# In the heads, TensorE turns a tile's own rows and makes its queries one head step sooner in its order

## What is computed

```
h = einsum('bnc,hdc->bhnd', x, Wh)            # 4 heads, 64 features
scores = where(mask, einsum('...nd,...md->...nm', h, h), NEG)
out_h = einsum('...nm,...md->...nd', softmax(scores), h) + bh
z = leaky_relu(concat_heads(out_h), 0.2)
h2 = einsum('bnk,dk->bnd', z, Wo)             # goes on to a second attention
```

## Time and profile before

| | |
|---|---|
| median of 3 runs | 1794.92 us (1794.16 to 1799.05) |
| the profiled execution | 1795.05 us |
| its span, first to last instruction | 1793.2 us |
| granted TensorE clock, mean over the span | 0.858 |
| PE busy | 1080.2 us, 60% |
| DVE busy | 1308.8 us, 73% |
| POOL busy | 1035.0 us, 58% |
| ACT busy | 784.8 us, 44% |

### The profile page before, as it was taken

How to read it: one execution, slowest core, us unless ns; L and a number is a source line. 1 busy time by engine, 2 the same in 40 slices (tenths; PEclk the granted TensorE clock), 3 DMA queues, 4 the chain that set the end, 5 groups by cost and what they waited for, 6 DMA issues and landing times.

```text
span 1793.2 us, 13782 instructions
## 1 busy us (share of the span) xinstructions
PE 1080.2 (60%) x3144; PEld 558.8 (31%) x3144; DVE 1308.8 (73%) x1699; ACT 784.8 (44%) x2502; POOL 1035.0 (58%) x939
## 2 busy tenths in 40 slices
PE   0000255365289899869999985646534777764673
PEld 0000132122144444434444441212113444542231
DVE  7987456789699997994768505999976986734462
ACT  0400253334247566544655652536433546643131
POOL 0084437641167788657686656877744865415882
PEclk9999988687699899979999998877775889876886
DMA  9260547431222122101111004442204543206666
GB/s 339 74 117 20 198 153 207 136 114 48 94 62 80 41 66 64 53 12 30 42 41 36 12 12 143 131 114 84 87 24 138 149 137 96 70 34 186 199 186 160
DMA packets 101626, 178.81 MB, mean 100 GB/s; under 512 B 47552, under 2 KB 56032, under 8 KB 99232
## 3 DMA queue, kind: packets, MB, share of 16 engines
q0 software_dynamic: 30960, 102.92, 19.9%
q1 hardware_dynamic: 51216, 70.05, 11.8%
q10 hardware_dynamic: 19360, 4.87, 1.6%
HBM read 147.88 MB, written 34.12 MB: 101 GB/s over the span
## 4 chain that ended last, share of the span: by engine, by line
DVE 30%; PE 29%; POOL 19%; issue 11%; ACT 5%; DMA 4%; DVEq 0%; POOLq 0%; ACTq 0%; SPq 0%
PE PS L1230 15%; POOL big L654 10%; DVE big L1691 5%; DVE big L1683 3%; PE PS L1176 3%; PE PS L1254 2%; PE PS L1290 2%; ACT big L897 2%; PE PS L1242 2%; DVE big L1687 2%; DVE big L1570 2%; POOL big L682 2%; DVE big L1617 2%; DVE stats L1613 2%; DVE big L1489 2%
## 5 line engine op out<-in xcount | busy, mean ns | idle before, releaser
L1230 PE MATMUL PS<-big,ident 128*128 128x512 f32 x1044 | 507.5, 637 | 107.1 <-ACT big L897 45.2
L897 ACT ACTIVATE big<-big 128x64 f32<-128x64 f32 x1632 | 404.7, 339 | 241.8 <-DVE big L1648 202.6
L682 POOL TENSOR_TENSOR big<-big 128x512 f32<-128x512 f32 x356 | 361.5, 1045 | 134.8 <-DVE big L1648 113.0
L1230 PEld LDWEIGHTS PS<-big,ident 128*128 128x128 f32 x1044 | 209.7, 206 | 367.4 <-issue 269.4
L1691 DVE TENSOR_REDUCE big<-big 128x32 f32<-128x2048 f32 (+4 forms) x126 | 297.7, 2362 | 4.3
L1214 PE MATMUL PS<-big,ident 128*128 128x512 f32 x348 | 190.3, 708 | 153.7 <-ACT big L897 85.8
L1683 DVE TENSOR_TENSOR big<-big,PS 128x2048 f32<-128x2048 f32 (+4 forms) x84 | 198.5, 2363 | 80.9 <-PE PS L1242 78.1
L654 POOL DMA_INDIRECT big<-tab,SI x142 | 174.2, 1227 | 117.7 <-PE PS L1214 40.9
L1176 PE MATMUL PS<-ident,big 128*128 128x128 f32 x640 | 105.8, 295 | 167.8 <-DMA big<-h_rows 67.8
L689 POOL TENSOR_TENSOR big<-big 128x512 f32<-128x512 f32 x64 | 81.5, 1273 | 147.7 <-ACT big L970 147.3
L654 POOL DMA_INDIRECT big<-h_rows,SI x142 | 138.4, 974 | 44.7 <-issue 27.2
(11 more groups left out here) (159 smaller groups left out, 1534.7 us busy)
## 6 DMA issues: line engine op xcount, KB each, us to landing
big<-in_adj SPq DMA_DIRECT2D x16, 1024.0 KB, 6.1
tab<-big SPq DMA_DIRECT2D x64, 132.0 KB, 1.8
big<-tab SPq DMA_DIRECT2D x32, 264.0 KB, 3.3
h_rows<-big SPq DMA_DIRECT2D x32, 256.0 KB, 2.0
big<-h_rows SPq DMA_DIRECT2D x32, 256.0 KB, 2.8
big<-in_x ACTq DMA_DIRECT2D x16, 256.0 KB, 5.0
big<-xs SPq DMA_DIRECT2D x4, 1024.0 KB, 9.4
h_table<-big SPq DMA_DIRECT2D x16, 256.0 KB, 2.0
```

Source lines behind the costliest of these rows:

```text
L682: ins = pool.tensor_tensor(bd(wbuf[:, i % NWB, j, :]), bd(rows[:, k + j, :]), over_d(S[:, h, k + j, :], B), ALU.mult)
L897: ins = act.activation(to, row, ACT.Copy, scale=S[:, h, k + j, b:b + 1])
L1230: mm = pe.matmul(to, ident[:, :], wbuf[:, i % NWB, k, :], start=(u != 2 and c == 0 and k == 0), stop=(c == len(parts) - 1 and k == n - f - 1))
```

## The change

On PE the turn of a tile's own rows goes from the end of step 4t - 2 to the end of step 4t - 3, `queries(t, 0)` from the start of step 4t - 1 to that of 4t - 2, and `queries(t, 1)` from the start of step 4t to that of 4t - 1. On ACT the copy of the turned own rows goes from step 4t - 1 to step 4t - 2, at the same place in the step. Both loops start at -3 instead of -2, for tile 0. No instruction is added or taken away, and all waits keep their values.

```diff
 # ACT
-                for m in range(-2, NT * HEADS + 10):
+                for m in range(-3, NT * HEADS + 10):
...
-                    if (m + 1) % HEADS == 0 and (m + 1) // HEADS < NT:
-                        t = (m + 1) // HEADS
+                    if (m + 2) % HEADS == 0 and (m + 2) // HEADS < NT:
+                        t = (m + 2) // HEADS
                         act.wait_ge(own_turned, t + 1)
 # PE
-                for m in range(-2, NT * HEADS + 10):
-                    if m >= 0 and m % HEADS == 0 and m // HEADS < NT:
-                        queries(m // HEADS, 1)
+                for m in range(-3, NT * HEADS + 10):
                     if (m + 1) % HEADS == 0 and (m + 1) // HEADS < NT:
-                        queries((m + 1) // HEADS, 0)
+                        queries((m + 1) // HEADS, 1)
+                    if (m + 2) % HEADS == 0 and (m + 2) // HEADS < NT:
+                        queries((m + 2) // HEADS, 0)
                     if 0 <= m - 5 < NT * HEADS:
...
-                    if (m + 2) % HEADS == 0 and (m + 2) // HEADS < NT:
-                        t = (m + 2) // HEADS
+                    if (m + 3) % HEADS == 0 and (m + 3) // HEADS < NT:
+                        t = (m + 3) // HEADS
                         pe.wait_ge(self_loaded[t % NRB], 16 * ((NT + t) // NRB + 1))
                         if t >= 1:
                             pe.wait_ge(q_used, 2 * (t - 1) + 1)
```

## The result

| | before | after |
|---|---|---|
| median | 1796.86 us (4 runs, 1794.16 to 1799.05) | 1819.59 us (4 runs, 1818.58 to 1821.29) |
| span of the profiled execution | 1793.2 us | 1819.5 us |
| mean granted clock | 0.858 | 0.861 |

The ratio of after to before is 1.0128, 95% interval 1.0109 to 1.0147: the change makes the kernel 20 to 26 us slower, 23.0 us at the middle. The forecast was +22.5 us.

What follows compares the result with a forecast made beforehand. PE sets the pace in the heads' two dense stretches, DVE between them through tiles 4 and 8. Terms 8.0 + 2.7 + 5.6 + 1.7 + 6.0 + 0.5 - 2.0 = +22.5 us give 1817 us, range 1804 to 1825.

Steps and rivals of the forecast that it cites:

- tile 3, up to q(5): DVE at tile 3: multiplication can start sooner, but divide(1, 2) waits for an exponential now behind more queries; +0.5 us.
- tile 5, q(5) to s16: PE at tile 5: queries waiting for DVE now stand ahead of job 14's sum, so its step follows the wait; +5.6 us.
- holes of tiles 6, 7, and tile 8's queries, s16 to s26: PE: uncovered waits for ACT's copy at tiles 6 and 7, 2.7 us; tile 8's queries before job 26's sum, 1.7.
- DVE through tile 8, s26 to q(9): DVE at tile 8: sooner queries allow one multiplication sooner, then a longer wait at divide; no term in the sum.
- tile 9, q(9) to s32: PE at tile 9: queries waiting for DVE now stand ahead of job 30's step, so it follows the wait; +6.0 us.
- holes of tiles 10 to 15, s32 to s63: PE at steps 4t, tiles 10 to 15: queries no longer cover the wait for ACT's copy, 6 x 1.34 = 8.0 us.
- the clock, within tiles 5 and 9: PE at half clock after the long idles: no hole behind the queries shortens it, gain 1.3 to 3.7 us, 2.0 taken.
- the luck of tile 3's `lower`: DVE operations slowed by POOL at tile 3: realignment gains none, since ACT's exponential caps it, or loses up to 5 us.
- What the waits should show: PE's waits for DVE grow, DVE's shift from queries to exponential, 1.2 us idle at steps 4t, sums of jobs 14, 30 later.
- Sooner queries pay: Rival: DVE's waits for queries at tiles 3 and 8 shrink, 1786 us; decided by tile 7's exponential start; chance 0.07.
- Hidden: Rival: PE's idle 4.55 + 16.15 us at the tile 5 and 9 waits absorbs the shifts, 1795 +- 5; chance 0.05.
- Only the blocked steps, or only the holes: Rival: just one loss occurs, steps put behind DVE waits (1806 us) or uncovered waits for ACT's copy (1805); chance 0.08.

Runs made afterwards that it cites:

- e7: Kernel before, with ACT taking tile 7's exponential at the start of step 31 instead of 32: 1795.81 us, ratio 0.9987.
- e12: Kernel before, own turn and its copy sooner, ACT's sum copy ahead of h2 copies and exponential, second-half queries of tiles 5, 9 a step later: 1774.98 us, ratio 0.9888.
- e8: Kernel before, with only the own rows' turn on PE and its ACT copy one step sooner, both query halves unmoved: 1785.01 us, ratio 0.9916.
- e1: Kernel after, with the second half of the queries, queries(t, 1), back in its old place at all tiles: 1797.75 us, ratio 0.9989.
- e6: Kernel after, with ACT taking tile 7's exponential at the start of step 31 instead of 32: 1811.32 us, ratio 1.0060.
- e3: Kernel after, with queries(t, 1) of tiles 5 and 9 alone back in their old place: 1811.86 us, ratio 1.0069.
- e11: Kernel after, with queries(t, 1) back in their old place at all tiles except 5 and 9: 1801.80 us, ratio 1.0028.
- e4: Kernel after, with ACT's copy of the sum put ahead of its two copies for h2 in a step: 1797.51 us, ratio 0.9994.

## Why the prediction was right, by its own steps

| term | predicted | measured in the profiles |
|---|---|---|
| tile 3, up to q(5) | +0.5 | 117.5 - 116.1 = +1.4 |
| tile 5, q(5) to s16 | +5.6, less its part of the clock's gain | 17.2 - 13.5 = +3.7 |
| holes of tiles 6, 7, and tile 8's queries, s16 to s26 | 2.7 + 1.7 = +4.4 | 107.2 - 102.6 = +4.6 |
| DVE through tile 8, s26 to q(9) | 0 | 61.3 - 61.2 = +0.1 |
| tile 9, q(9) to s32 | +6.0, less its part of the clock's gain | 21.8 - 17.8 = +4.0 |
| holes of tiles 10 to 15, s32 to s63 | +8.0 | 280.0 - 272.2 = +7.8 |
| the clock, within tiles 5 and 9 | -2.0 | -3.3 (of it -1.6 at tile 5, which e7 shows to be chance) |
| stage | +22.5 | +21.6 |

**The clock** was the term most off, by 1.3 us, and within its range (1.3 to 3.7). Queries and sums behind the two waits lost 3.78 - 1.89 and 3.73 - 3.60, and 3.78 - 1.89 and 6.44 - 5.31, in all 5.0 us at the lower level (1.2 GHz), against 8.3 before. The forecast had taken 4.6 to 7 us at that level behind each wait; its rows show the 4.6 alone, and nothing shows the 7. Measured, the granted clock stood at half for 3.8 and 5.8 us behind the two waits, and for 8.5 and 12.0 before. With 3.3 put back, tiles 5 and 9 come to 3.7 + 4.0 + 3.3 = 11.0 us against the 11.6 of the sum. Half of the gain is luck. e7 is the kernel before but for one exponential at step 31, far behind tile 5. It has the same idle time and the same hole there, and yet its sum of job 15 (L1232 here) takes 3.70 us, not 5.29:

```profile
595.64 3.78 PE L1244 MATMUL PS<-MB,big 128*128 128x256 f32 x8 [4.55 <-DVE big L1685]
600.95 3.70 PE L1232 MATMUL PS<-big,ident 128*128 128x512 f32 x8 [1.52 <-ACT big L960]
```

So the same work loses 1.6 us more or less to the clock from one profile to the next, and against a profile of before like e7's at tile 5 the stage would have lost 23.2 us, not 21.6 (an estimate from these two rows). At tile 9 the gain holds in every profile but e12's, whose order is another: the sum of six slots behind the wait took 7.02 to 8.25 us in the 8 profiles with a hole of 2.33 to 2.81 us ahead of it, and 5.31 to 6.46 in the 5 with none, whatever the idle time before the queries (9.25 to 23.73 us). No run moved the hole alone.

**The holes of tiles 10 to 15** came out at 7.8 us for 8.0, but not as six times 1.34. Tiles 11 to 15 cost 1.44 us each and tile 10 cost 0.6, since the queries of tile 10 had waited 2.10 us behind the turn before and waited 1.25 after. The prediction had put that difference at zero for all tiles.

**Tile 3** was right in kind and 0.9 us off. DVE did start sooner, and waited 3.23 us for the exponential at `divide(1, 2)`, where before it hadn't waited. The cap on the luck of tile 3's `lower` held too. There the collisions came out smaller (3.97 and 0.29 us against 3.03 and 4.00), yet the divide behind was not sooner:

```profile
566.29 0.38 DVE L1646 TENSOR_REDUCE mx<-big 128x32 f32<-128x128 f32 x1 [2.51 <-ACT big L879]
```

DVE waited 2.51 us for ACT's exponential, so most of the 2.8 us that were saved in `lower` was lost again at once. So the range, worked out from the row of ACT's exponential and not from the rule of the exclusive lock, was the right one for the change. In e8 the divide did not wait for the exponential, and there the missing collision was worth 3.8 us less the 1.4 us of the wait behind it. The collision rows agree with the Trainium skill (SBUF — State Buffer, section "SBUF: two separate sides") in that an operation of 0.29 us took up to 4.00 while POOL ran; that it was the lock no run here isolated. They do not fit it in one thing: by a lock that is held for one instruction the wait would end with that instruction, and here DVE's operation (556.08 to 560.08) ends 0.16 us behind three of POOL in a row, before:

```profile
556.65 1.28 POOL L689 TENSOR_TENSOR big<-big 128x512 f32<-128x512 f32 x1
557.88 2.04 POOL L682 TENSOR_TENSOR big<-big 128x512 f32<-128x512 f32 x2
```

**What the waits should show** was right in direction and wrong in one size. PE's wait for DVE was to grow from 22.3 to some 35 us, about 10 at tile 5 and 25 at tile 9. It was 7.41 and 17.24, and 4.27 more at the turn of tile 9's own rows, which now reaches DVE's work too early. The forecast had not taken off the holes and the later queries that hold PE itself up ahead of these waits. It had no part in the sum. The other signs came as forecast: idle time of 1.17 or 1.18 us ahead of the sum at the steps 4t, and the sums of jobs 15 and 31 later than before (610.77 against 601.38, 799.21 against 780.05).

**The rivals.** Sooner queries pay: refuted by e1, and by e6 in its condition: there tile 7's exponential starts no later than before (236.2 us from the first turn against 236.9), DVE gains 10 us against the kernel after, and the kernel is still 11 to 13 us slower than before. Hidden: refuted by the table. Only the blocked steps, or only the holes: both are there, e3 and e11 have one each (13.9 and 6.8 us in the stage).

**What stays open:** what holds the sums at steps 4t + 1 in e4, and why a hole behind a long wait costs clock at tile 9. That e11's ratio gives 5.0 us and its stage 6.8 needs no cause: its interval is 2.2 to 7.9 us.

## What to carry to other kernels

A long wait that one engine has for another is worth only the time to the next wait behind it: look one instruction further, at what that waits for, before you move its source. In an order written by hand an instruction also has a use as a filler. Where an engine sets the pace, moving work out of a hole costs the hole, and moving it in front of a wait puts everything behind it on the far side; so take the wait's end from the trace and count the work that had been done before it. Turn the finding round: what leaves a hole on the engine that sets the pace (here a copy queued behind less urgent ones, and a turn followed at once by what needs its copy) is where the gain lies, here 1.5%.

## What the runs showed of the hardware that had not been expected

Half clock after a wait cost less at tile 9 when the work behind it was unbroken. Before, a hole of 2.81 us stood between queries and sum, and the sum of six slots took 8.12 us; after, with no hole and with 17.24 us of idle time ahead, it took 6.44, and the 13 profiles counted above say the same. A single profile can mislead here: at tile 5 the four-slot sum took 5.29 us before and 3.70 in e7, behind the same hole and the same idle time. A small DVE operation that meets POOL's work moved between 0.29 and 4.00 us with shifts of a few us elsewhere, and one such meeting made 2.4 to 3.8 of the 13.6 us that e8 gained in the stage. At 4.00 us such an operation lasted longer than one instruction of POOL beside it (1.28).
